# Reordering the last program of a graph and expert network: where VectorE adds the second layer's experts, where TensorE applies attention, and where ScalarE computes its exponentials

## The reference, cut to what matters

```python
x = x + L0_gnn(layernorm(x), adj, ...)        # dense neighbour sum and a small network
x = x + L0_ffn(layernorm(x), edge_index, ...) # 524288 edges choose 2 of 4 experts for each node
x = x + L1_gnn(layernorm(x), adj, ...)        # softmax attention within a tile, then elu
x = x + L1_ffn(layernorm(x), ...)             # 2 of 8 experts for each node
```

```python
h = input @ W
e = leaky_relu(einsum('bnf,f->bn', h, a1 + a2))[:, :, None]
att = softmax(where(adj > 0, e, NEG), axis=2)
x = x + elu(einsum('bij,bjf->bif', att, h))
...
probs = softmax(xf @ gate_w + gate_b)          # 8 experts, the best 2 are kept
for each expert: out += cw[:, None] * (gelu(xf @ w1 + b1) @ w2 + b2)
```

## Time and profile before

| what | value |
|---|---|
| median of 3 runs | 3447.95 us |
| lowest and highest run | 3446.22 and 3448.56 us |
| the profiled execution, first to last instruction (its own time) | 3672.8 us |
| PE busy / DVE busy / ACT busy / POOL busy | 70% / 75% / 47% / 32% |
| mean granted TensorE clock | 0.833 of 2.4 GHz |

### The profile page before, as it was taken

How to read it: one execution, slowest core, us unless ns; L and a number is a source line. 1 busy time by engine, 2 the same in 40 slices (tenths; PEclk the granted TensorE clock), 3 DMA queues, 4 the chain that set the end, 5 groups by cost and what they waited for, 6 DMA issues and landing times.

```text
span 3672.8 us, 49655 instructions
## 1 busy us (share of the span) xinstructions
PE 2583.2 (70%) x15405; PEld 1913.6 (52%) x15406; DVE 2761.0 (75%) x8069; ACT 1723.5 (47%) x3052; POOL 1169.0 (32%) x1205
## 2 busy tenths in 40 slices
PE   1888888888888612026777777777777777777889
PEld 0666656656666401014555555555555555555666
DVE  7888778887887546367877777787787787788774
ACT  1566566665665311124454444454444544545544
POOL 0000000000000037655554545555545545555200
PEclk7899999998999855557887877878888788788899
DMA  2111111111110223223223223332232322322200
GB/s 84 34 48 47 44 46 50 44 43 38 50 38 32 72 59 77 49 62 76 63 59 78 61 63 73 66 75 65 58 78 65 73 66 62 75 64 59 76 12 9
DMA packets 228561, 210.53 MB, mean 57 GB/s; under 512 B 70781, under 2 KB 160585, under 8 KB 227657
## 3 DMA queue, kind: packets, MB, share of 16 engines
q1 hardware_dynamic: 190008, 190.83, 17.6%
q0 software_dynamic: 37280, 14.38, 4.5%
q10 hardware_dynamic: 1008, 2.15, 0.2%
HBM read 159.49 MB, written 47.74 MB: 56 GB/s over the span
## 4 chain that ended last, share of the span: by engine, by line
DVE 31%; PE 13%; another core or an unknown queue 8%; issue 8%; POOL 1%; ACT 1%; DVEq 0%; SPq 0%; DMA 0%; POOLq 0%; ACTq 0%
DVE keep_x L2174 7%; PE lay_b_y L1800 6%; PE lay_b_z L1791 5%; DVE lay_oh L1055 2%; POOL lay_got L1754 1%; DVE lay_oht L2079 1%; DVE lay_xn L2209 1%; DVE lay_parts L1068 1%; DVE lay_left L1067 1%; DVE lay_parts L1069 1%; DVE lay_parts L1066 1%; DVE lay_msg L1063 1%; DVE lay_stats L2198 1%; DVE lay_hp L2236 1%
## 5 line engine op out<-in xcount | busy, mean ns | idle before, releaser
L1754 POOL DMA_INDIRECT lay_got<-node_table,lay_idx x1152 | 1145.5, 994 | 928.6 <-PE lay_b_z L1791 326.3
L1800 PEld LDWEIGHTS lay_b_y<-lay_w,lay_hid 128*128 128x128 f32 x4096 | 572.1, 215 | 284.9 <-issue 271.4
L1800 PE MATMUL lay_b_y<-lay_w,lay_hid 128*128 128x128 f32 x4096 | 576.9, 298 | 114.8 <-issue 66.1
L1791 PE MATMUL lay_b_z<-lay_xin,lay_w 128*128 128x512 f32 x1024 | 599.8, 715 | 18.2 <-ACT lay_hid L1945 9.2
L1945 ACT ACTIVATE lay_hid<-lay_b_z,lay_b 128x512 f32<-128x512 f32 x512 | 332.6, 683 | 530.1 <-PE lay_b_z L1791 305.3
L2174 DVE SCALAR_TENSOR_TENSOR keep_x<-lay_b_y,lay_gates,keep_x 128x128 f32<-128x128 f32 x1024 | 287.4, 343 | 273.3 <-remote 175.4
L879 POOL MEMSET find_no_src<- 128x9 int32 x1 | 0.1, 108 | 1252.5 <-POOLq L47 1252.5
L2023 ACT ACTIVATE lay_unused<-lay_hub_wide,lay_halves 128x1152 bf16<-128x1152 uint16 x256 | 320.3, 1251 | 124.5 <-DMA lay_hub_wide<-sorted_dst 100.7
L461 PE MATMUL front_b_h<-front_xt,front_m 128*128 128x512 f32 x512 | 273.6, 666 | 58.8 <-ACT front_act_m L571 30.6
L1791 PEld LDWEIGHTS lay_b_z<-lay_xin,lay_w 128*128 128x128 f32 x1024 | 205.1, 223 | 189.3 <-issue 164.0
L217 DVE TENSOR_TENSOR sort_keys<-sort_keys 128x1024 f32<-128x1024 f32 (+2 forms) x182 | 257.4, 1414 | 37.9 <-ACT sort_keys L539 35.4
(11 more groups left out here) (392 smaller groups left out, 4577.3 us busy)
## 6 DMA issues: line engine op xcount, KB each, us to landing
lay_wide<-sorted_dst SPq DMA_DIRECT2D x128, 288.0 KB
lay_hub_wide<-sorted_dst SPq DMA_DIRECT2D x128, 288.0 KB
made<-front_y SPq DMA_DIRECT2D x128, 256.0 KB, 2.0
lay_y<-made SPq DMA_DIRECT2D x32, 1024.0 KB
lay_got<-node_table,lay_idx POOLq DMA_INDIRECT x1152
front_adj<-in_adj SPq DMA_DIRECT2D x32, 256.0 KB, 3.1
keep_x<-in_x SPq DMA_DIRECT2D x32, 256.0 KB, 3.5
lay_adj<-in_adj SPq DMA_DIRECT2D x32, 256.0 KB
```

The source lines that it names most:

```text
L1754: pool.indirect_dma_start(out=got[:, b % RING, c, :], out_offset=None, in_=table, in_offset=bass.IndirectOffsetOnAxis(ap=idx[:, b % AHEAD, ...
L1791: pe.matmul(b_z[c][:, :], w1[:, e, P * c:P * c + P], flat(xin[g % 2][:, :, :]), start=True, stop=True).then_inc(z_done, 1)
L1800: mm = pe.matmul(b_y[n % 2][:, P * j:P * j + P], hid[n % 2][:, c, P * j:P * j + P], w2[:, e * HK + c, :], start=(c == 0), stop=(c == HK - 1))
```

## The change

No instruction is added or removed; only the order within each engine's list changes. The `count_rest` and `rest_hots_of` loops, which only matter in iterations -1 and 0, are wrapped in functions and stay where they were.

- VectorE: L1 expert 0 is added right after `choose(f)` in the first quarter, ahead of the L0 experts 0 and 1; L1 expert 1 follows them, ahead of `elu`; L1 expert 2 goes between `end_elu` and `norms`, expert 3 behind `norms` (both second quarter); expert 4 behind `shift` and expert 5 behind `scores` (third quarter); experts 6 and 7 behind `weigh` (fourth quarter). Before, experts 0 and 1 followed `norms`, 2, 3 and 4 were in the third quarter and 5, 6 and 7 in the fourth.
- TensorE: `turn_att` moves from the end of an iteration into the first quarter of the next one, behind expert 0; `apply_att` moves from the iteration's start to behind expert 1. Expert 1 moves from the second quarter to the first, `bias(0, m)` behind expert 0.
- ScalarE: the GELU of `expert(f, 0)` goes ahead of `keep_att`, `exp_hm` moves behind the second GELU and `keep_gates(1, f)`, and the GELU of `expert(f, 7)` goes ahead of the exponentials at the iteration's end.

```diff
 TensorE
-                apply_att(t)
-                turn_gates(0, m)
-                attend(b)
-                bias(0, m)
-
-                expert(f, 0)
+                attend(b)
+                counts(i, 0)
+                turn_gates(0, m)
+                expert(f, 0)
+                turn_att(t)
+                bias(0, m)
+                expert(f, 1)
+                apply_att(t)
+
                 attend(b + 1)
-                expert(f, 1)
+                counts(i, 1)
                 turn_gates(1, f)
                 expert(f, 2)
                 turn_x2(t)
                 expert(f, 3)
                 logits(t)
...
                 expert(f, 7)
-                turn_att(m)
 ScalarE
+                keep_gates(0, m)
+                expert(f, 0)
                 keep_att(t)
-                keep_gates(0, m)
-                exp_hm(t)
                 count(b)
-                expert(f, 0)
                 expert(f, 1)
                 keep_gates(1, f)
+                exp_hm(t)
                 count(b + 1)
...
                 expert(f, 6)
-                exp_att(m)
+                expert(f, 7)
                 exp_logits(t)
                 if i % QUAD == QUAD - 1 and 0 <= i < groups:
                     exp_scores(i // QUAD)
-                expert(f, 7)
+                exp_att(m)
                 count(b + 3)
 VectorE
                 attend(b)
+                choose(f)
+                expert(1, f, 0)
                 expert(0, m, 0)
+                expert(0, m, 1)
+                expert(1, f, 1)
                 elu(t)
-                expert(0, m, 1)
-                choose(f)
                 expert(0, m, 2)
 
                 attend(b + 1)
                 expert(0, m, 3)
                 bias(0, m)
                 end_elu(t)
+                expert(1, f, 2)
                 norms(t)
-                expert(1, f, 0)
-                expert(1, f, 1)
+                expert(1, f, 3)
 
                 attend(b + 2)
-                expert(1, f, 2)
                 shift(t)
-                expert(1, f, 3)
+                expert(1, f, 4)
                 if quad:
                     scores(i // QUAD)
-                expert(1, f, 4)
+                expert(1, f, 5)
 
                 attend(b + 3)
-                expert(1, f, 5)
                 weigh(m)
                 expert(1, f, 6)
                 expert(1, f, 7)
```

More of the change, by code:

```diff
@@ L1892, in logits, with counts @@
                 mm.then_inc(logit_done, 1)
+            def counts(i, quarter):
+                if i < 1:
+                    for n in (2 * quarter, 2 * quarter + 1):
+                        count_rest(8 * i + 8 + n)
             look_up(0)
@@ L1919, in _ @@
                 attend(b + 2)
-                if i < 1:
-                    for n in (4, 5):
-                        count_rest(8 * i + 8 + n)
+                counts(i, 2)
                 expert(f, 4)
@@ L1930, in _ @@
                 attend(b + 3)
-                if i < 1:
-                    for n in (6, 7):
-                        count_rest(8 * i + 8 + n)
+                counts(i, 3)
                 expert(f, 7)
-                turn_att(m)
         @block.scalar
@@ L2102, in rest_hots_of, with hots_of_rest @@
                 ins.then_inc(rest_ready, 1)
+            def hots_of_rest(i, quarter):
+                if i < 1:
+                    for n in (2 * quarter, 2 * quarter + 1):
+                        rest_hots_of(8 * i + 8 + n)
             def scores(q):
@@ L2289, in _ @@
                 attend(b)
-                if i < 1:
-                    for n in (0, 1):
-                        rest_hots_of(8 * i + 8 + n)
+                hots_of_rest(i, 0)
+                choose(f)
+                expert(1, f, 0)
                 expert(0, m, 0)
+                expert(0, m, 1)
+                expert(1, f, 1)
                 elu(t)
-                expert(0, m, 1)
-                choose(f)
                 expert(0, m, 2)
                 attend(b + 1)
-                if i < 1:
-                    for n in (2, 3):
-                        rest_hots_of(8 * i + 8 + n)
+                hots_of_rest(i, 1)
                 expert(0, m, 3)
```

14 lines of the change are left out of this document (2 added, 12 removed).

## The result

| | before | changed |
|---|---|---|
| median of 4 runs each, same chip | 3447.09 us (3446.22 to 3448.56) | 4115.4 us (4112.15 to 4117.65) |
| ratio | | 1.193, interval 1.1917 to 1.1951 |
| profiled execution, span | 3672.8 us | 4114.3 us |

The change makes the kernel 668 us slower. I had said slower, by 497 us, with 4090 us as the upper end.

A forecast was written before the change was run, and what follows sets the result against it. Bound: VectorE's work plus, at places, waits for TensorE's matmuls. (21.2 us of new waits + 13.6 of restarts) x 14 pairs = 487, plus 10 for iterations 32 to 35, on 3447.95: 3945 us; range 3670 to 4090.

The forecast's parts named there:

- expert 0: First quarter: TensorE needs 4.6 us after the one-hots, VectorE has only `choose`, 3.25; new wait 1.35 us.
- expert 3: Behind `norms`: `turn_x2` waits for `xn2`, then `up` and `down`; 4.05 - 1.05 = 3.0 us of wait, the most trusted.
- expert 4: Third quarter, behind the one-hots: TensorE 4.15 us against `shift`, 0.65; wait 3.5 us.
- expert 5: Third quarter: TensorE's chain 5.15 us against one addition, 1.06; wait 4.1 us in even iterations, none in odd ones.
- the signs named beforehand: New profile: waits in quarters one to three, none at experts 6 and 7, pairs 150 us or more, clock 0.50, more PE.
- the price of a restart: Clock falls while TensorE idles before four stretches an iteration: 1.7 us each (0 to 3.4), eight a pair, 13.6 us.
- `end_elu` and expert 2: Second quarter: `turn_gates`, `up`, `down` take 4.05 us behind `bias(0, m)` against `end_elu`, 0.7; wait 3.35 us, covering ScalarE's exponential.
- the sum's zero for expert 7: Fourth quarter: ready 4.15 us behind the one-hots, against `weigh` and one addition, 4.5; no wait.
- the undisturbed pair of 120.5 us: Kernel before, two iterations without inflated waits: 57.7 + 62.8 us, 9.2 of it waits; taken for the timed runs.
- the long waits were real: Rival: timed runs have the 130.9 us pair, so less is added: 3609 us, 3799 with restarts; chance 0.1 below 3700.
- The clock rival: Spread experts keep TensorE at 2.4 GHz, only 21.2 us a pair remain: 307 us more, 3755 us; chance 0.2.
- The table switch: ScalarE before `end_elu`: exponential 1.29 us after the table instruction, not the skill's 2.66, which would add some 28 us.

The follow-up runs named there:

- experiment 6: Changed kernel with L1 additions spread a quarter behind TensorE's reordered experts, attention and `exp_hm` back as before; ratios to the kernel before 1.0153, 1.018, 0.9719 on three chips.
- experiment 5: Changed kernel plus never-read matmuls filling TensorE's idle times: first try (into `b_z`) 4284.4 us; second (into `b_y`, fewer calls) 4151.4 us, ratio 1.134.

## Why the prediction was right in kind and short in size

**Right: the mechanism and the waits behind a warm TensorE.** The forecast said that each early addition waits until the chain from the handshake to `down` is through, and by how much. For expert 1 I had 1.95 us and the row shows 1.86; for expert 5, 4.1 and 4.20, and it is absent in odd iterations as said. VectorE without waits was to be 50.3 and 61.0 us; 78.87 us less 28.5 of waits is 50.4, and 88.38 less 27.0 is 61.4. Moving back attention or ScalarE's order changes nothing; one addition a handshake later gives back 139 us; the order of experiment 6 gives back all but 55 and 66 us on two chips and more than all on a third. Of the signs named beforehand the waits, the pair above 150 us and the clock at 0.50 came; the waits for expert 7 are gone in even iterations only; the chain cannot be read, as the page's chain of the changed kernel breaks off after 1% of the span.

**Failed: the price of a restart.** The step was "the nearest rows give 1.7, one of the two", that is, only one of `up` and `down` at 1.2 GHz. In the changed kernel the transposes ahead of `up`, `up` itself and, in three of the four places, a part of `down` run at the lower clock: from 2805.53 to the end of `down` at 2812.49 it is 6.96 us against 4.05 at full clock, from 2819.73 to 2826.48 it is 6.75 against 4.05, from 2832.34 to 2839.47 it is 7.13 against 4.15. In the waits, measured less forecast, that is

| wait | forecast at full clock | measured even / odd | more |
|---|---|---|---|
| expert 0 | 1.35 | 3.6 / 3.2 | 2.3 / 1.9 |
| `end_elu` and expert 2 | 3.35 | 6.6 / 6.4 | 3.3 / 3.1 |
| expert 3 | 3.0 | 5.9 / 5.8 | 2.9 / 2.8 |
| expert 4 | 3.5 | 6.7 / 6.7 | 3.2 / 3.2 |

22.7 us a pair in eight restarts, 2.8 each instead of 1.7. The rows from which I took 1.7 had idle times of 1.6 and 2.7 us ahead of them; in the new order it is 2.98 and 1.66 in a row, 5.91, or 7.24, and more of each chain is slow. I had named that difference (4 to 8 us) and not used it. That the longer idle time is what makes the restart longer fits these rows, but no run varied it by itself; that the clock is the cost, experiment 5 shows. The upper end of the range took 3.0 a restart, but no missed one with it.

**Failed: the sum's zero for expert 7 ("No wait").** In odd iterations `scores` holds VectorE so long that TensorE has run out of work at the fourth handshake: it idles 5.63 us before `attend` at 2766.03, its `up` at 2768.68 takes 3.76 us, and VectorE waits 2.64 us for expert 7 at 2775.16. The prediction put 4.15 us of TensorE against 4.5 of VectorE there; the restart made the 4.15 into 6.84. It is a ninth restart, and the sum had eight. The sum of the two: 8 x (2.8 - 1.7) + 2.6 = 11.4 us a pair, 160 us in 14 pairs, of the 170 us between 3945 and 4115.4. The measured time is 25 us above the upper end of the range, less than the 37 us of the missed wait.

**Right, with a wrong reason: the undisturbed pair of 120.5 us.** I called the late releases of the profile of before something that the profiled execution had and the timed runs had not. They are a matter of the chip: on three of the four chips of the experiments the timed runs of before take 3649 to 3691 us too. The profile shown, 3672.8 us, looks like one of these, while the times shown are of the other kind. As the base of the sum 120.5 fits the result's chip, though it was worked out from the wrong premise and one even iteration: experiment 6 gains 95.2 us over the kernel before on such a chip, and its mean pair of 114.3 us would make that 14 x (120.5 - 114.3) = 87. No trace of the kernel before on such a chip was taken, so the pair itself was not measured. The rival "the long waits were real" was true for three chips, but it fails as a price: it expected a smaller loss where the late releases are real, and on the second chip the change costs 654 us, on the result's 668. The changed kernel has late releases there too; its mean pair is 177.3 us against 167.2.

**The clock rival falls.** Windows at 0.50 stand at the places foretold. The Trainium skill (TensorE: Matmul & The Clock Gate, HAM oscillation) describes a kernel whose bursts of matmuls are shorter than the waits between them and start at the throttled clock each time. The trace agrees as to the start, with `up` at 3.62, 3.62 and 3.76 us in the rows of PE above, though here the burst may be the longer of the two: from 2832.34 the matmuls run for 17 us, behind idle times of 2.98 and 1.66.

**The table switch was rightly taken from the row.** In the changed kernel it is again 1.29 us from the table instruction to the exponential (timeline of ScalarE):

```profile
2806.58 0.59 ACT L1959 ACTIVATE lay_gate_t<-lay_b_b 8x512 f32<-8x512 f32 x1 [12.23 <-PE lay_b_b L1832]
2807.19 1.28 ACT L1971 ACT_TABLE_LOAD   x1
2808.48 0.63 ACT L1971 ACTIVATE lay_hm<-lay_hm 128x512 f32<-128x512 f32 x1
```

The Trainium skill (ScalarE: Activation LUTs, What ACT_TABLE_LOAD costs) makes up its 2.66 us from a load of about 1283 ns and a drain of about 1380. The 1.28 us of the row agree with the load; no drain is seen ahead of the exponential, and `end_elu` does not end behind expert 2.

## What to carry to other kernels

When two engines hand work to each other through lists in a fixed order, place a use at least one handshake behind its making: asked for in the same quarter, a result cost its chain less what little work the asking engine had beside it; asked for a quarter later, the same spreading gained 2.8% on one chip and lost 1.5 and 1.8% on two others. Price a short chain behind an idle TensorE at the lower clock from its first matmul to its last but a part (here 2.8 us more on 4.05 to 4.6), when the idle time is longer than in the rows at hand. Compare a profile's own time with the times that it stands beside before reading its waits: a gap of 6% may be another chip, and an order that wins on one can lose on the other.

## What the runs showed of the hardware that I had not expected

One program on one core takes 3446 to 3452 us on the fourth chip and 3649 to 3691 on three others. In the traces the difference shows as results of TensorE that come late. VectorE's waits of 0.3 us or more from 1500 us on that are put down to "remote" add up to nothing in the two traces of the faster kind (the changed kernel on the result's chip, experiment 6 on the fourth), and to 161 to 364 us in each of the eleven from the three slower chips; the profile of before has 221. Of each of these twelve sums 127 to 287 us stand at the L1 additions, which wait only for engines of the same core; there "remote" can be no outside queue. Windows of experiment 6 on the third chip, 6.7 us of such a stretch and the 5.3 us behind it:

```profile
2827.00:2833.70 6.70, 6.70 (x49) 4.79 (x49) 5.20 (x17) 1.37 (x2) 4.68 (x5) 1.00 0.28 52
2833.70:2839.00 5.30, 2.77 (x17) 2.20 (x15) 0.00 (x0) 0.00 (x0) 3.83 (x5) 0.98 0.11 9
```

The granted clock is 1.00 and 0.98, but 15 weight loads are recorded in 5.3 us, where the stretch before has 49 in 6.7; one `down` is spread from 2833.71 to about 2839, against 1.95 us on the fourth chip. VectorE gets its look-ups, which the timeline ends at 2831.66, at 2840.75. It also waits for the gathered rows of the block there, but ScalarE, whose copy of `b_g` waits for TensorE's transposes alone (they end at 2832.15), starts at the same moment:

```profile
2840.75 0.27 DVE L1060 TENSOR_REDUCE lay_look<-lay_b_att 128x36 f32<-128x108 f32 x1 [7.40 <-issue]
2840.76 0.60 ACT L1985 ACTIVATE lay_xt<-lay_b_g 128x512 f32<-128x512 f32 x1 [10.93 <-remote]
```

This would also explain "remote" in the earlier trace rows and at 2893.16 above: the output comes later than the modelled end of its matmuls (2891.11 for the latter). It goes with the two misses on such chips: keeping TensorE busy gained about half of what was expected, with 2 us of lateness ahead of expert 5, and experiment 6 has waits of this kind up to 8 us long there, though not only these: its pairs also show a lower mean granted clock, 0.76 and 0.79 in two windows against 0.86 and 0.93. What holds TensorE back was not found. In the stretch shown the granted clock does not show it, and a late supply of its instructions or operands was not looked into. The Trainium skill (TensorE: Matmul & The Clock Gate, Seeing it yourself) tells of a limit of the current that takes a die to 13/16 of the clock when three of its cores run dense matmuls; that would show as a granted clock of 0.81 within a stretch and this kernel uses one core, so no run here shows it to be the same.
